# Feed-forward weights loaded behind the tokens, and quantised ahead of the tokens instead of after them

## What is computed

```python
xn = layernorm(x)                                   # 2048 x 128
qkv = xn @ w_attn + b_attn                          # 16 heads of 8
scores = q @ k.T * 8 ** -0.5 + power_law_mask       # a query sees itself and later keys
att = softmax(scores) @ v @ w_proj + b_proj
h = silu(fp4(xn) @ fp4(w_gate).T) * (fp4(xn) @ fp4(w_up).T)     # 352 wide
out = x + att + fp4(h) @ fp4(w_down).T
```

## Time and profile before

| | |
|---|---|
| three runs | 621.84, 622.52, 622.91 us |
| profiled execution, its own time | 622.93 us |
| its span (first to last instruction) | 621.2 us |
| busy: PE, DVE, POOL, ACT | 558.1, 551.6, 540.7, 400.7 us |
| granted TensorE clock, mean | 0.987 |

### The profile page before, as it was taken

One profiled execution on the slowest core, in us unless ns is written; L12 is line 12 of the kernel. 1 busy time (PEld: TensorE's weight loads), 2 busy tenths in 40 slices (PEclk: granted clock), 3 DMA queues, 4 the chain that ended last, 5 costly groups with the idle time before them and its releaser, 6 DMA issues.

```text
span 621.2 us, 11230 instructions
## 1 busy us (share of the span) xinstructions
PE 558.1 (90%) x3746; PEld 252.1 (41%) x3797; DVE 551.6 (89%) x1165; ACT 400.7 (65%) x868; POOL 540.7 (87%) x409
## 2 busy tenths in 40 slices
PE   5999498999898989998989898988989898998885
PEld 4677364444343424333423333342334343332323
DVE  5999498999999999899999989998999999997662
ACT  4677337676766666656667575667656667668793
POOL 7378669989999999898999999999988898897983
PEclk9999889999999999999999999999999999999997
DMA  5334442201000001100000000000000000000000
GB/s 154 103 98 110 137 76 70 60 35 46 2 3 1 1 2 50 45 1 2 2 2 0 19 1 1 2 2 1 2 2 1 19 0 2 1 1 2 1 2 18
DMA packets 14833, 16.68 MB, mean 27 GB/s; under 512 B 1639, under 2 KB 14216, under 8 KB 14360
## 3 DMA queue, kind: packets, MB, share of 16 engines
q1 hardware_dynamic: 14240, 15.70, 9.1%
q10 hardware_dynamic: 536, 0.26, 0.2%
HBM read 11.75 MB, written 4.01 MB: 25 GB/s over the span
## 4 chain that ended last, share of the span: by engine, by line
PE 47%; POOL 22%; DVE 11%; ACT 9%; issue 5%; SPq 4%; DMA 1%; ACTq 1%; POOLq 0%; another core or an unknown queue 0%; DVEq 0%
POOL ring L894 16%; PE psum L1465 13%; PE psum L1423 10%; PE psum L1447 8%; DVE mxp L1238 6%; ACT ring L1048 2%; PE psum L1398 2%; PE psum L1379 2%; POOL xw L912 2%; POOL xw L910 2%; DVE ring L1265 2%; PE psum L1381 2%; PE psum L1450 1%; POOL xw L914 1%; SPq L666 1%
## 5 line engine op out<-in xcount | busy, mean ns | idle before, releaser
L894 POOL TENSOR_TENSOR ring<-ring,dist 128x1024 f32<-128x1024 f32 (+3 forms) x223 | 436.9, 1988 | 36.5 <-ACT ring L1048 36.2
L1238 DVE TENSOR_REDUCE mxp<-psum 128x1 f32<-128x512 f32 (+3 forms) x640 | 355.3, 601 | 21.2 <-PE psum L1423 16.8
L1048 ACT ACTIVATE ring<-psum 128x512 f32<-128x512 f32 (+3 forms) x446 | 212.0, 529 | 121.9 <-PE psum L1450 68.1
L1423 PE MATMUL psum<-kop,qop 96*128 96x512 bf16 (+3 forms) x640 | 199.7, 352 | 5.7 <-DVE mxp L1238 2.5
L1447 PE MATMUL psum<-qop,kop 128*128 128x512 bf16 (+3 forms) x590 | 178.0, 346 | 18.0 <-DVE mxp L1238 11.4
L1465 PE MATMUL psum<-ring,vaug 128*32 128x512 f32 (+3 forms) x1280 | 150.0, 539 | 15.1 <-POOL ring L894 13.3
L1265 DVE TENSOR_TENSOR ring<-psum,dist 128x512 f32<-128x512 f32 (+3 forms) x194 | 116.7, 627 | 12.7 <-ACT psum L1048 12.5
L1048 ACT ACTIVATE psum<-psum 128x512 f32<-128x512 f32 (+3 forms) x194 | 101.0, 552 | 35.3 <-PE psum L1450 15.9
L1423 PEld LDWEIGHTS psum<-kop,qop 96*128 96x128 bf16 x640 | 57.9, 98 | 123.2 <-DVE mxp L1238 41.0
L1447 PEld LDWEIGHTS psum<-qop,kop 128*128 128x128 bf16 x640 | 59.5, 97 | 91.1 <-DVE mxp L1238 24.4
L1426 PE MATMUL psum<-tri_q,identb 128*128 128x128 bf16 x256 | 55.9, 221 | 0.0
(11 more groups left out here) (134 smaller groups left out, 468.4 us busy)
## 6 DMA issues: line engine op xcount, KB each, us to landing
parts_dram<-qpart SPq DMA_DIRECT2D x18, 128.0 KB, 3.2
kop<-parts_dram SPq DMA_DIRECT2D x6, 384.0 KB
qop<-parts_dram SPq DMA_DIRECT2D x6, 384.0 KB
xin<-_attn_hidden_states_dram SPq DMA_DIRECT2D x4, 256.0 KB, 4.9
ring<-inv_dram SPq DMA_DIRECT2D x1, 1024.0 KB, 4.9
out_dram<-xin SPq DMA_DIRECT2D x4, 256.0 KB, 2.3
qop<-parts_dram SPq DMA_DIRECT2D x3, 288.0 KB
kop<-parts_dram SPq DMA_DIRECT2D x3, 288.0 KB
```

The costliest lines, as they stand in the source:

```text
L894: g_.tensor_tensor(slot(p)[:, :, 0:n], slot(p)[:, :, 0:n], both, ALU.mult).then_inc(weighed_pool, 1)
L1048: a_.activation(scores if pair_vec[p] else slot(p)[:, e % 2, 0:n], scores, ACT.Exp, scale=SCALE).then_inc(exp_done, 1)
L1238: v_.tensor_reduce(mxp[:, u % 2, 4 * a + j, c - g:c - g + 1], bank(*o)[:, 0:n], AX_X, ALU.max).then_inc(max_used, 1)
L1423: ins = mm(bank(*o)[:, 0:n], qop[0:K_MAX, u // NQ % 2, h, P * a:P * (a + 1)], kop[0:K_MAX, h, k0:k0 + n], start=True, stop=(c != g))
```

## The change

The eight weight DMAs are moved from behind chunk 2's `kop` loads to the place right behind the store of the inverse distances, before SP waits for that store. The numbers of the pieces are changed, so that the three weights are quantised first and the four chunks of tokens after them; the planner's due time for the weights becomes 9500 ns. POOL zeroes only the part of w_gate's and w_up's third block that no load fills (partitions 96 to 127, 2 x 128 columns), so that loads and zeroing touch different bytes; DVE now waits for this zeroing (semaphore `zeroed`) where SP did before. The opening transposes go from 20 to 14. All orders that the planner writes follow from the new numbers.

```diff
--- before.py
+++ after.py
@@ -30,15 +30,15 @@
 FCH = [(0, 128), (128, 128), (256, 96)]
 XW = S + 6 * P + F
 SC_COLS = 35
-W_PIECES = [4, 5, 6]
-X_PIECES = [0, 1, 2, 3]
+W_PIECES = [0, 1, 2]
+X_PIECES = [3, 4, 5, 6]
 PIECES = {n: (S + 3 * P * k, (3 * P, 3 * P, F)[k]) for k, n in enumerate(W_PIECES)}
 PIECES.update({n: (S - GQ * (k + 1), GQ) for k, n in enumerate(X_PIECES)})
 VC = HD + 1
 SLOTS = 8
 BANKS = 7
 OUT_BANK = 7
-WARM = 20
+WARM = 14
 NEG = -1e30
 EPS = 1e-5
 BELOW_TIE = 1.0 - 3 * 2.0 ** -23
@@ -62,7 +62,7 @@
 POOL_QUEUE, LAST_QUEUE = 3800, 1500
 MROWS = 3
 FILL = 200
-WEIGHTS_AT = 62000
+WEIGHTS_AT = 9500
 
 SEEN = 60
 PV_SWITCH = 310
@@ -156,7 +156,7 @@
         for k in range(FP4_STAGES):
             needs = [("DVE", ("fp4", n, k - 1))] if k else [
                 ("PE", ("xnT", X_PIECES.index(n))) if n in X_PIECES else ("DMA", ("weights",))]
-            needs += [("DVE", ("rest", 1, 1))] if n == k == 0 else []
+            needs += [("DVE", ("rest", 1, 1))] if n == X_PIECES[0] and k == 0 else []
             needs += [("POOL", ("fp4", n - 1, 1))] if k == 5 and n else []
             w = PIECES[n][1]
             vec(("fp4", n, k), (w, 64, 220, w, w, w)[k], needs, rank=HELD_RANK if k >= 3 else FP4_RANK)
@@ -736,6 +736,15 @@
                              ).then_inc(x_loaded[c], 16)
             sp.wait_ge(inv_ready, 1)
             sp.dma_start(inv_dram.rearrange("(p n) -> p n", p=P), invd[:]).then_inc(inv_stored, 16)
+            for m, w in enumerate((w_gate, w_up)):
+                o = S + 3 * P * m
+                sp.dma_start(xw[:, o:o + 2 * P].rearrange("p (t k) -> p t k", t=2),
+                             w[0:2 * P, :].rearrange("(t p) k -> p t k", p=P)).then_inc(w_loaded, 16)
+                sp.dma_start(xw[0:F - 2 * P, o + 2 * P:o + 3 * P], w[2 * P:F, :]).then_inc(w_loaded, 16)
+            sp.dma_start(xw[:, S + 6 * P:XW], w_down).then_inc(w_loaded, 16)
+            sp.dma_start(wp[:], w_proj).then_inc(w_loaded, 16)
+            sp.dma_start(bv[:], b_attn[2 * D:3 * D].rearrange("(p o) -> p o", o=1)).then_inc(late_loaded, 16)
+            sp.dma_start(wdT[F - 2 * P:F - 2 * P + 1, 2], b_proj.rearrange("(a n) -> a n", a=1)).then_inc(late_loaded, 16)
             sp.wait_ge(inv_stored, 16)
             sp.dma_start(hankel, bass.AP(inv_dram.tensor, 0, [[1, P], [1, S]])).then_inc(hankel_loaded, 16)
             for ci, c in enumerate(CHUNKS):
@@ -769,17 +778,6 @@
                         load_k(sp, c, 4, NH, kop_loaded[c])
                     else:
                         load_k(sp, c, 0, NH, kop_loaded[c])
-                    if c == GROUPS[1]:
-                        sp.wait_ge(zeroed, 1)
-                        for m, w in enumerate((w_gate, w_up)):
-                            o = S + 3 * P * m
-                            sp.dma_start(xw[:, o:o + 2 * P].rearrange("p (t k) -> p t k", t=2),
-                                         w[0:2 * P, :].rearrange("(t p) k -> p t k", p=P)).then_inc(w_loaded, 16)
-                            sp.dma_start(xw[0:F - 2 * P, o + 2 * P:o + 3 * P], w[2 * P:F, :]).then_inc(w_loaded, 16)
-                        sp.dma_start(xw[:, S + 6 * P:XW], w_down).then_inc(w_loaded, 16)
-                        sp.dma_start(wp[:], w_proj).then_inc(w_loaded, 16)
-                        sp.dma_start(bv[:], b_attn[2 * D:3 * D].rearrange("(p o) -> p o", o=1)).then_inc(late_loaded, 16)
-                        sp.dma_start(wdT[F - 2 * P:F - 2 * P + 1, 2], b_proj.rearrange("(a n) -> a n", a=1)).then_inc(late_loaded, 16)
 
             for o in orders["SP"]:
                 if o[0] == "q":
@@ -842,7 +840,10 @@
             heads = vaug[:, :, 0:VC * NH].rearrange("p t (h e) -> p t h e", e=VC)
             g_.memset(heads[:, :, :, HD:VC], 1.0).then_inc(vones_ready, 1)
             g_.memset(vaug[:, :, VC * NH:], 1.0).then_inc(vones_ready, 1)
-            g_.memset(xw[:, S:S + 6 * P], 0.0).then_inc(zeroed, 1)
+            pool.wait_ge(vones_ready, 2)
+            third = xw[F - 2 * P:P, S:S + 6 * P].rearrange("p (m t k) -> p m t k", m=2, t=3)[:, :, 2]
+            g_.memset(third, 0.0).then_inc(zeroed, 1)
+            pool.wait_ge(zeroed, 1)
 
             for o in orders["POOL"]:
                 if o[0] == "split":
@@ -1135,6 +1136,7 @@
                     vec.wait_ge(scales_zeroed, 1)
                     if n in W_PIECES:
                         vec.wait_ge(w_loaded, 16 * N_W)
+                        vec.wait_ge(zeroed, 1)
                     else:
                         vec.wait_ge(xnT_psum, X_PIECES.index(n) + 1)
                     ins = v_.tensor_reduce(amax[:, n, 0:nb], blocks, AX_X, ALU.max, apply_absolute_value=True)
```

## The result

The changed kernel takes 608.75 us (median of 4 runs, 608.19 to 609.90) against 622.57 us for the kernel before (4 runs). The ratio is 0.9782, 95% interval 0.9765 to 0.9799: 13.6 us less. The forecast was 612.6 us, 9.9 less, in a range of 607.5 to 618.0.

What follows compares the result with a forecast made beforehand. DVE's time was taken as the bound, with PE and POOL nearly as full. Idle time removed, 7.97 + 1.5 + 0.5 = 9.9 us, took the profiled 622.93 to 613.0, less 0.4 for the median: 612.6 us, range 607.5 to 618.0.

Steps and rivals of the forecast that it cites:

- The bound and the stall: Whole kernel: it runs on DVE's time; DVE's 7.97 us wait for w_proj, up to 75.69 us, goes away.
- The DMAs in their new place: SP's queue at the start: eight weight DMAs issued by about 8.4 us, landed between 9.4 and 12.8; cost zero.
- Rival 3: Opening loads: the queue is stuck here too, weights land at 20.7, DVE stands 8.6 us longer; 621.2 us, chance 0.06.
- The wait for the zeroing: DVE's first weight stage waits for POOL's zeroing until 12.1; DVE stands 3.7 us instead of 5.17, won 1.5.
- The quantisation in the gaps: Opening: weight stages fill DVE's gaps, half of 0.99 us won; chain to first maxima up to 2.8 us late, not lost.
- The opening transposes: Start of PE's work: six fewer bring q and k 1.36 us earlier, worth zero because DVE is on the weights.
- The sum: DVE's idle time that goes away: 7.97 + 1.5 + 0.5 = 9.9 us; forecast 612.6 us, chance 0.50.
- rival 2: DVE's 3.36 us of idle gaps between 88 and 100 us go too, as the clock stays up; 609.2 us, chance 0.14.
- Rival 1: Start of main loop: the late chain to the first product with v sets the pace, gain 5.2 us; 617.3, chance 0.26.
- Rival 4: Opening: 14 transposes too few to raise TensorE's clock, low until 26 us; 3.1 us slower, 625.6, chance 0.04.

Runs made afterwards that it cites:

- e1: Changed kernel with the pieces numbered as before (tokens quantised first, weights last), loads still early; 612.55 us, ratio 0.9835 to the kernel before.
- e3b: Changed kernel with POOL's zeroing moved from behind its last constants to behind the identity; 606.97 us, ratio 0.9741 to the kernel before.
- e2: Changed kernel with 20 opening transposes again instead of 14; 608.53 us, ratio 0.9774 to the kernel before.
- e7: Changed kernel with the planner constant SEEN at 61 ns instead of 60, which alters only the planned order; ratio 0.9814 to the kernel before.
- e12: Changed kernel with the planner constant SEEN at 59 ns instead of 60; ratio 0.9872 to the kernel before.
- e4: Changed kernel with the planner's due time for the weights at 12500 ns instead of 9500; 611.25 us, ratio 0.9823 to the kernel before.
- e6: Changed kernel with only w_gate quantised ahead of the tokens, w_up and w_down after them; 611.91 us, ratio 0.9828 to the kernel before.
- e5: Kernel before with only the planner's due time for the weights changed, 76000 ns instead of 62000; 614.59 us, ratio 0.9871.

## Why the prediction was right, point by point

- **The bound and the stall: right.** DVE's idle time was the right account. In the order of before, the loads ahead and 14 transposes gave 10.3 us for 10.65 us of DVE's time (e1). The stall itself was priced a little low: 1.3 us of the gaps behind it went with it in the changed kernel and 1.7 in e1, which the sum had at nothing.
- **The DMAs in their new place: right.** Landing at 9.7 us, in the lower part of 9.4 to 12.8; the load of the shifted distances was issued at 8.25 (8.4 forecast). Rival 3, the stuck queue, did not come: each of the six issues took 0.43 to 0.67 us.
- **The wait for the zeroing: right.** 12.37 for 12.1, DVE idle 4.18 us for 3.7. That this wait and not the load decides was confirmed by e3b, in which DVE starts at 9.78. The step won 1.0 us, not 1.5.
- **The quantisation in the gaps: right in kind, the lateness too small.** First "rest" at 15.64 for 15.3. The chain to the first maxima became 4.9 us late (28.75 against 23.85), where "up to 2.8 us late" stood. Missing was PE: it stands behind DVE's weights, its granted clock falls, and that was some 1.4 us (e2). Lateness is free only as long as DVE has other work. In the profiled execution it had not always: DVE did 1.2 us less between 17.9 and 67.6 than before. In e2, e7 and e12 the chain was 3.2 to 3.6 us late and DVE lost nothing there, as was forecast.
- **The opening transposes: right.** Nothing to be seen with the weights first (e2); 0.3 to 1.4 us of DVE's idle time with the tokens first.
- **The sum: 9.9 us of DVE time, measured 9.84 by 100 us; the time fell by 13.6.** The 9.84 is in part luck, since 1.2 us lost before 67.6 and 1.3 us won behind the stall cancel. The step that failed is the sentence that "a new order of everything behind moves waits about by a microsecond or two". The new order took 1.0 us of work from DVE and 2.1 us of idle time after 100 us, and e7 and e12, one nanosecond away in a constant, give 11.6 and 8.0 us where the changed kernel gives 13.6. The three have a mean of 11.1. So that term was mis-sized by two or more, it also held work and not only waits, and luck had a good part in the 608.75. This time is below even rival 2's 609.2, and inside the range only by the margin that was added for the order.
- **Rival 1 (the first product with v): wrong**, though its sign in the profile came, a product only 2.6 us earlier. e1 has that product at 75.6 and is slower. An early first product is no gain if DVE's quantisation is still to do.
- **Rival 2 (the gaps between 88 and 100 go too): its number was near, its reason was not.** Of the 3.36 us, 1.3 went. The rest of what lies beyond the sum came after 100 us, from the new order.
- **Rival 4 (the clock): its mechanism is there, its price is not.** In the changed kernel's profile the low level came as a stretch of three microseconds after PE had stood still. In e12, with the same 14 transposes, the products for q and k took 3.69 us where they take 1.96 before and in the changed kernel. The same came in e4, e6 and e7 (3.75 each), so in four of the nine profiled kernels with 14 transposes and in none of the five with 20. Timeline of PE in e12:

```profile
5.68 3.25 PE L1301 MATMUL psum<-identf 128*128 128x128 f32 x14 [5.68 <-POOL identb L819]
8.72 1.06 PE L1319 MATMUL psum<-identf,xw 128*128 128x128 f32 x4
10.56 3.69 PE L1329 MATMUL psum<-xnT,wa 128*128 128x512 f32 x4 [0.78 <-ACT xnT L950]
```

  So 14 are sometimes too few. DVE's weights hide it: e12's DVE has done more by 100 us than the changed kernel (11.1 against 9.8). All this is far from the 11.6 us of work at which it would have decided. The Trainium skill, "TensorE: Matmul & The Clock Gate", Part 4 (PE-mode transpose), has it that transposes do not count for the full clock; e5's 20 took 3.80 us where all at the low level take 4.53, with nothing but transposes ahead of them, and that speaks against it.

## What to carry to other kernels

In a kernel whose order is planned, a due time that is wrong for one transfer can cost several microseconds, and one number may mend much of it (8.0 us in e5): compare due times with the landings in the trace before moving any load. Count a gain as what the busiest engine has done more by a fixed time; lateness of a chain costs nothing while that engine has other work. See also whether the planner gave that engine more work in all, as in e12 and e5. When an edit changes a whole planned order, shake a harmless constant and time that too, and test a single step with the order held fixed, as in e1 and e3b, or a few microseconds of chance will be taken for its effect.

## What the runs showed of the hardware

Opening transposes of the same shape took different times in different executions of the same 20: 4.53 us in the profile before, 4.19 in e2, 3.80 in e5, so the rise of TensorE's clock falls at a different point of the burst each time. With it the wait of DVE for q and k moved, 5.17 us before and 4.2 in e5, with nothing of the opening changed. A standstill of PE of 3.54 us was followed by a low stretch (granted clock 0.59 over 3.3 us), one of 2.17 us was not. And a queue that was stuck for 7.42 us behind loads of `kop` took the same eight DMAs behind 1 MB of tokens without being stuck; why was not tried.
